# Masks over pairs of tiles, six of them in stage one, eight more split blocks and four kept blocks, in a two-layer graph kernel on one core

## Chip, cores and metric

One core of a Trainium2 chip runs the whole program. The metric is the device time of one execution in microseconds, lower is better.

## Reference

Two graph layers over 4096 nodes with 128 features, each followed by a residual and a layer norm without scale or shift. `adj` is 4096 x 4096, mostly zeros, with entries from 0.05 to 1.

```python
def reference(x, adj, L0_gnn_W1, L0_gnn_W2, L0_gnn_b, L1_gnn_W, L1_gnn_B):
    # layer 0:  K = 16 mixtures
    node = x @ W1                                  # (n, K)
    hw = einsum('nc,kcf->nkf', x, W2)
    x0 = einsum('nk,nkf->nf', node, hw)
    x1 = _layernorm(x + relu(adj @ x0 + node @ b))
    # layer 1
    msg = x1 @ W + B
    sens = exp(-(1.0 / adj - 1.0) ** 2 / 0.5)
    weights = where(adj < 1.0, sens, 0.0)
    return _layernorm(x1 + weights @ msg)
```

## The kernel before

Everything is kept transposed (features on partitions). `adj` is cut into 8 x 8 blocks of 512 x 512. It is read twice: as *row tiles* i = 0 to 63 (row r = i // 8, block g = i % 8) for `adj @ x0`, and as *weight tiles* t = 0 to 63 (column c = t // 8, block j = t % 8) for `weights @ msg`. Each tile is a 128 x 2048 array of 1 MB.

Stage one computes x0 for 8 groups of 512 nodes. TensorE makes the products `hw` in PSUM; for half of the chunks VectorE multiplies and adds them over k (`sum_over_k`, L861 and L864, PSUM and `part_acc` as operands), for the other half ScalarE scales them into `prods` (L600) and GpSimd adds these in a tree (`fold`, L1315, SBUF operands only). TensorE writes the first half's products into four banks, so it can be two quarters of a group ahead of VectorE. GpSimd also makes the remainder `x_lo` of the next group (L1323).

After that TensorE runs one fixed list of steps i. In each step it does row tile i and, 13 steps later than its own number (COL_LAG), column tile t = i - 13. A row tile is either four full-precision products (L451; two matmuls each, so eight in the profile) or, where `is_split` holds, *split*: VectorE rounds the tile to fp32r (`adj_hi`, L895) and subtracts (`row_lo`, L897), and TensorE does twelve one-pass matmuls (L440 to L442). `adj_hi` has two buffers, so `split_row_tile` waits until the row tile two splits back is done. When a row is complete, `node_bias` (L457) closes it, then come `residual` (L922), `centre` (L463 and L464 in two passes, L467 in full precision), `variance` (L473, L474 or L477), `scale_row` (L948), `messages` (L483), `copy_messages` (L966) and `add_row` (L957, a copy at L953 for kept blocks). For rows in ROWS_TWO_PASS, `round_row`, `remainder_of_row` (L934), `round_square` and `remainder_of_square` split the operands first.

A weight tile passes through VectorE `mask` (L909), then ScalarE `take_ln` (L616), `take_inverse` (L621), `take_square` (ScalarE L626, or VectorE L915 for every second pair) and `take_exp` (L633, L636). From tile 6 on, ScalarE works over two tiles at once. Column tiles of kept blocks add up in their own PSUM bank; for the others a shared bank is taken, and VectorE adds it to `sumT` (`add_part`, L974 a copy, L980 an addition).

The order on VectorE and ScalarE is a list of calls written out by hand. All loads go through SP's queue in a fixed order: row tile i + 5 once row tile i is done, weight tile t + 10 once column tile t is done; the weight slots 6 to 9 overlap stage one's arrays and are loaded after steps 2, 4, 7 and 9 (LATE_AT).

Of the kernel before, what the change touches and what calls it, by code (L numbers as in the profile page):

```python
# [5 lines left out]
F32 = mybir.dt.float32  # L6
# [5 lines left out]
P = 128  # L12
# [9 lines left out]
KEPT = 2  # L22
L1_BANKS = 2
# [5 lines left out]
SPLIT = (1, 3, 4, 5, 7)  # L29
SPLIT_FIRST = ((3, 5, 7), (1, 3, 5, 7))  # L30
SPLIT_LAST = (1, 3, 4, 5, 7)
# [10 lines left out]
ROWS_TWO_PASS = (2, 6)  # L42
# [23 lines left out]
def gnn_kernel(nc, adjT, xT, W1, W1T, W2, b0, WT, BT, outT):  # L66
# [23 lines left out]
    def is_split(i):  # L90
        if i // NB == NB - 1:
            return i % NB in SPLIT_LAST
        return i % NB in (SPLIT_FIRST[i // NB] if i < 2 * NB else SPLIT)

# [28 lines left out]

    def is_added(t):
        return t % NB >= KEPT or t >= TILES - NB

    def added_to(t):
        return len([s for s in range(t + 1) if is_added(s)])

# [7 lines left out]
    shared = [t for t in range(TILES) if t % NB >= KEPT]  # L137
# [10 lines left out]
    with ExitStack() as ctx:  # L148
# [9 lines left out]
        x0 = sb("x0", [P, NB * CH, P])  # L158
        if SPLIT:
            x0_hi = sb("x0_hi", [P, len(SPLIT) * CH, P], F32R)  # L160
            x0_lo = sb("x0_lo", [P, len(SPLIT) * CH, P], F32R)
# [44 lines left out]
        x1T = y  # L206
# [15 lines left out]
        yc_ps = psum("yc_ps", [P, BW])  # L222
        var_ps = psum("var_ps", [P, BW])
        small_ps = acc_ps[:, 1, P:4 * P].rearrange("p (n f) -> p n f", f=P)
        msg_ps = var_ps.rearrange("p (c f) -> p c f", f=P)
        shared_ps = [l1_ps[:, 0, :], l1_ps[:, 1, :], acc_ps[:, 0, :]]
        var2_banks = [var_ps[:, :], acc_ps[:, 1, :], yc_ps[:, :]]
# [85 lines left out]
        def _(sp):  # L313
# [34 lines left out]
            for g in (2, 3):  # L348
                load_x(g)
            for i in range(ROW_RING):  # L350
                load_row_tile(i)
            for t in range(WT_RING - LATE_SLOTS):
                load_wt(t)
# [25 lines left out]
        def _(pe):  # L379
# [48 lines left out]
            def row_tile(i):  # L428
                r, g = i // NB, i % NB
                acc = acc_ps[:, r % 2, :]  # L430
                if g == 0:
                    at_least(pe, y_made, r - 1)
                if is_split(i):
# [4 lines left out]
                    for c in range(CH):  # L438
# [3 lines left out]
                        mm = pe.matmul(acc, x0_lo[:, k, :], hi[:, c, :], start=False, stop=False)  # L442
# [16 lines left out]
            def centre(r):  # L459
                if row_in_two_pass(r):  # L460
                    pe.wait_ge(rounded_w_made, 2)
                    pe.wait_ge(y_lo_made, r - ROWS_TWO_PASS[0] + 1)
                    pe.matmul(yc_ps[:, :], centre_r[:, :], y_hi[:, :], start=True, stop=False)  # L463
                    pe.matmul(yc_ps[:, :], centre_r[:, :], y_lo[:, :], start=False, stop=True).then_inc(yc_made, 1)  # L464
                    return
                pe.wait_ge(y_made, r + 1)
                pe.matmul(yc_ps[:, :], centre_w[:, :], y[:, :], start=True, stop=True).then_inc(yc_made, 1)  # L467
# [11 lines left out]
            def messages(r):  # L479
                pe.wait_ge(x1_made, r + 1)  # L480
                pe.wait_ge(ln_var_made, r + 1)
                for c in range(CH):
                    mm = pe.matmul(msg_ps[:, c, :], x1T[:, c * P:(c + 1) * P], W_sb, start=True, stop=True)  # L483
                mm.then_inc(msg_made, 1)

            def col_tile(t):
# [3 lines left out]
                if j >= KEPT:  # L490
# [3 lines left out]
                    elif t >= THIRD_FROM:  # L494

                        pe.wait_ge(y_made, NB - 1)
                    out, first, last = shared_ps[bank_of[t]], True, True
                else:
                    out, first, last = kept_ps[:, j, :], c == 0, c == NB - 1
# [6 lines left out]
            def last_col_tile(half):  # L506

                pe.wait_ge(sum_added, added_to(before[LAST] if half == 0 else TILES - NB + 1))
# [27 lines left out]
            for i in range(LAST + COL_LAG):  # L536
# [7 lines left out]
                if g == 4 and 1 <= r < NB or i == TILES + 3:  # L544
# [4 lines left out]

                if g == 0 and 1 <= r <= NB and row_in_two_pass(r - 1):  # L550
# [14 lines left out]
        def _(act):  # L565
# [72 lines left out]
            def square(r):  # L638
                act.wait_ge(yc_made, r + 1)
                at_least(act, var_made, r)  # L640
                act.activation(sq[:, 0, :], yc_ps[:, :], ACT.Square).then_inc(sq_made, 1)
# [27 lines left out]
            round_x0(NB - 1)  # L669
            take_ln(0)  # L670
            take_inverse(0)
            take_square(0)
# [5 lines left out]
            square(0)  # L678
            take_exp(1)
            log_variance(0)  # L680
            take_inverse(2)
            inverse_root(0)
# [5 lines left out]
            take_ln(4)  # L688
            take_exp(3)
            take_inverse(4)  # L690
            take_square(4)
            take_ln(5)
            take_exp(4)
            take_inverse(5)
            take_square(5)
            take_ln(6)
            take_exp(5)
            take_inverse(6)
            square(1)
            take_square(6)  # L700
            take_ln(8)
            take_exp(6)
            log_variance(1)
            take_inverse(8)
            inverse_root(1)
            take_ln(10)
            take_inverse(10)
            take_exp(8)
            take_ln(12)
            take_square(10)  # L710
            take_inverse(12)
            take_exp(10)
            take_ln(14)
            take_exp(12)
            take_inverse(14)
            take_square(14)
            take_ln(16)
            square(2)
            take_exp(14)
            take_inverse(16)  # L720
            take_ln(18)
            log_variance(2)
            take_inverse(18)
            inverse_root(2)
            take_exp(16)
            take_ln(20)
            take_square(18)
            take_inverse(20)
            take_exp(18)
            take_ln(22)  # L730
            take_exp(20)
            take_inverse(22)
            take_square(22)
            take_ln(24)
            take_exp(22)
            square(3)
            take_inverse(24)
# [3 lines left out]
            take_exp(24)  # L741
            inverse_root(3)
            take_ln(28)
            take_square(26)
            take_inverse(28)
            take_exp(26)
            take_ln(30)
            take_inverse(30)
            take_exp(28)
            take_ln(32)  # L750
            take_square(30)
            take_inverse(32)
            square(4)
            take_exp(30)
            take_ln(34)
            take_exp(32)
            take_inverse(34)
            log_variance(4)
            take_square(34)
            inverse_root(4)  # L760
            take_exp(34)
# [600 lines left out]
```

## Time and profile before

| | before |
|---|---|
| time, median of 3 runs | 550.95 us (550.93 to 551.05) |
| the profiled execution: its time, its span | 552.33 us, 550.5 us |
| TensorE (PE) busy | 543.5 us, 99% |
| VectorE (DVE) busy | 497.3 us, 90% |
| ScalarE (ACT) busy | 497.2 us, 90% |
| GpSimd (POOL) busy | 83.3 us, 15% |
| mean DMA rate | 258 GB/s |

Busy shares are means over the span: GpSimd works in stage one alone (the first 104 us), ScalarE's weight work begins at 118.03 us. TensorE's matmuls are pipelined, and their modelled durations overlap, so tiles are measured here from one start to the next.

### The profile page before, as it was taken

How to read it: one execution, taken by the hardware profiler on the slowest of the kernel's cores; microseconds unless marked ns; L12 is line 12 of the kernel's file. 1: busy time of each engine (PE TensorE's matmuls, PEld its weight loads, DVE VectorE, ACT ScalarE, POOL GpSimd, SP SyncE). 2: the span in 40 equal slices, each digit the busy share in tenths (PEclk: the TensorE clock that was granted, in tenths of full speed). 3: DMA queues.
4: the chain of work that ended last, by engine and by line, in shares of the span. 5: the costliest groups of instructions: out<-in, count | busy, mean ns of one | idle time of the engine just before them, and what ended most of it. 6: DMA issues, size and time to landing. Idle time of an engine off the chain costs nothing.

```text
span 550.5 us, 5213 instructions
## 1 busy us (share of the span) xinstructions
PE 543.5 (99%) x1780; PEld 325.7 (59%) x1780; DVE 497.3 (90%) x564; ACT 497.2 (90%) x448; POOL 83.3 (15%) x76
## 2 busy tenths in 40 slices
PE   9999999999999999999999999999999999999996
PEld 7887888655655565556555655565555555554444
DVE  6686777999998799999989999999989998999997
ACT  5777888449999999989999999999999998999984
POOL 2888899400000000000000000000000000000000
PEclk9999999999999999999999999999999999999999
DMA  5992000299997888888888888887988796870003
GB/s 169 394 426 93 21 1 0 78 373 426 414 359 279 319 317 323 311 307 323 331 305 310 326 320 312 314 314 301 329 307 308 301 327 235 314 283 1 0 20 133
DMA packets 23130, 142.05 MB, mean 258 GB/s; under 512 B 2720, under 2 KB 3264, under 8 KB 6720
## 3 DMA queue, kind: packets, MB, share of 16 engines
q1 hardware_dynamic: 22960, 141.46, 68.5%
q8 instruction: 14, 0.23, 0.2%
q10 hardware_dynamic: 144, 0.26, 0.2%
q14 instruction: 12, 0.10, 0.1%
HBM read 139.62 MB, written 2.10 MB: 257 GB/s over the span
## 4 chain that ended last, share of the span: by engine, by line
PE 92%; DMA 4%; POOL 1%; issue 1%; ACT 1%; DVE 1%; DVEq 0%; ACTq 0%; POOLq 0%
PE l_ps L502 26%; PE acc_ps L451 17%; PE kept_ps L502 10%; PE acc_ps L442 6%; PE acc_ps L440 6%; PE acc_ps L441 6%; PE hw_ps L410 4%; DMA x_in<-xT_dram 4%; PE hw_ps L416 4%; PE hw_ps L413 4%; PE acc_ps L502 2%; PE var_ps L483 1%; PE acc_ps L457 1%; PE acc_ps L388 1%; POOL prods L1315 1%
## 5 line engine op out<-in xcount | busy, mean ns | idle before, releaser
L502 PE MATMUL l_ps<-wt_pair,msg 128*128 128x512 f32 x328 | 147.3, 592 | 0.0
L909 DVE SCALAR_TENSOR_TENSOR wt_pair<-wt_pair 128x2048 f32<-128x2048 f32 x60 | 136.5, 2285 | 3.5 <-DMA wt_pair<-adjT_dram 3.5
L616 ACT ACTIVATE wt_pair<-wt_pair 128x4096 f32<-128x4096 f32 (+1 forms) x33 | 109.0, 3302 | 10.9 <-DVE wt_pair L909 10.9
L621 ACT ACTIVATE wt_pair<-wt_pair 128x4096 f32<-128x4096 f32 (+1 forms) x33 | 109.0, 3302 | 0.3
L502 PEld LDWEIGHTS l_ps<-wt_pair,msg 128*128 128x128 f32 x328 | 61.7, 190 | 70.3 <-issue 69.2
L451 PE MATMUL acc_ps<-rows,x 128*128 128x512 f32 x216 | 96.8, 592 | 0.0
L600 ACT ACTIVATE prods<-hw_ps,node 128x128 f32<-128x128 f32 x256 | 73.1, 374 | 17.5 <-PE hw_ps L416 15.7
L897 DVE TENSOR_TENSOR row_lo<-rows,adj_hi 128x2048 fp32r<-128x2048 f32 x37 | 84.8, 2293 | 1.3
L864 DVE SCALAR_TENSOR_TENSOR part_acc<-hw_ps,node,part_acc 128x128 f32<-128x128 f32 x224 | 60.7, 343 | 21.1 <-PE hw_ps L416 21.1
L451 PEld LDWEIGHTS acc_ps<-rows,x 128*128 128x128 f32 x216 | 41.0, 190 | 50.1 <-issue 49.8
L440 PE MATMUL acc_ps<-adj_hi,x_hi 128*128 128x512 f32 x148 | 68.3, 462 | 0.0
L1315 POOL TENSOR_TENSOR prods<-prods 128x1024 f32<-128x1024 f32 (+2 forms) x45 | 66.4, 1477 | 10.8 <-ACT prods L600 8.3
L915 DVE SCALAR_TENSOR_TENSOR wt_pair<-wt_pair 128x4096 f32<-128x4096 f32 (+1 forms) x18 | 66.7, 3707 | 0.0
L442 PE MATMUL acc_ps<-adj_hi,x_lo 128*128 128x512 f32 x148 | 57.8, 391 | 0.0
L441 PE MATMUL acc_ps<-row_lo,x_hi 128*128 128x512 f32 x148 | 57.8, 390 | 0.0
L502 PE MATMUL kept_ps<-wt_pair,msg 128*128 128x512 f32 x128 | 57.4, 592 | 0.0
L633 ACT ACTIVATE wt_pair<-wt_pair 128x4096 f32<-128x4096 f32 (+1 forms) x18 | 54.8, 3043 | 1.6 <-DVE wt_pair L915 1.6
L895 DVE CAST adj_hi<-rows 128x2048 fp32r<-128x2048 f32 x37 | 45.2, 1222 | 11.4 <-PE acc_ps L442 9.4
L626 ACT ACTIVATE wt_pair<-wt_pair 128x4096 f32<-128x4096 f32 (+1 forms) x18 | 54.9, 3050 | 0.3
L636 ACT ACTIVATE wt_pair<-wt_pair 128x4096 f32<-128x4096 f32 (+1 forms) x18 | 54.7, 3041 | 0.0
L410 PE MATMUL hw_ps<-W_hi,x_hi 128*128 128x512 f32 x128 | 50.9, 397 | 1.2 <-ACT prods L600 1.2
L416 PE MATMUL hw_ps<-W_lo,x_hi 128*128 128x512 f32 x128 | 50.0, 391 | 0.0
(117 smaller groups left out, 554.7 us busy)
## 6 DMA issues: line engine op xcount, KB each, us to landing
rows<-adjT_dram SPq DMA_DIRECT2D x68, 1024.0 KB, 4.9
wt_pair<-adjT_dram SPq DMA_DIRECT2D x60, 1024.0 KB, 4.8
x_in<-xT_dram SPq DMA_DIRECT2D x8, 256.0 KB, 3.9
x_row<-xT_dram SPq DMA_DIRECT2D x8, 256.0 KB, 5.1
outT_dram<-sumT SPq DMA_DIRECT2D x7, 256.0 KB, 2.0
W_in<-W_dram SPq DMA_DIRECT2D x3, 256.0 KB, 4.5
W_in<-W_dram ACTq DMA_DIRECT2D x1, 256.0 KB, 3.7
outT_dram<-sumT SPq DMA_DIRECT2D x2, 128.0 KB, 1.9
```

Of the source, the lines that this page charges most:

```text
L410: pe.matmul(out, x_hi[:, s, nodes], W2_hi[:, ks, :], start=True, stop=False)
L416: pe.matmul(out, x_hi[:, s, nodes], W2_lo[:, ks, :], start=False, stop=True).then_inc(hw_made[half], 1)
L440: pe.matmul(acc, x0_hi[:, k, :], hi[:, c, :], start=(g == 0 and c == 0), stop=False)
L441: pe.matmul(acc, x0_hi[:, k, :], lo[:, c, :], start=False, stop=False)
L442: mm = pe.matmul(acc, x0_lo[:, k, :], hi[:, c, :], start=False, stop=False)
L451: mm = pe.matmul(acc, x0[:, g * CH + c, :], row_in[i % ROW_RING][:, c, :], start=(g == 0 and c == 0), stop=False)
L502: mm = pe.matmul(out, msg[:, c % 2, k, :], wt[t][:, k, :], start=(first and k == 0), stop=(last and k == CH - 1))
L600: op = act.activation(prods[:, c2, k, :], hw_ps[1][:, n % HW_BANKS[1], kk, :], ACT.Copy, scale=node[:, s, HALF + c2, k:k + 1])
L616: act.activation(w, w, ACT.Ln, bias=TINY).then_inc(ln_made, 1)
L621: act.activation(w, w, ACT.Exp, scale=-1.0).then_inc(inv_made, 1)
L897: dve.tensor_tensor(flat(lo[:, :, :]), flat(whole[:, :, :]), flat(hi[:, :, :]), ALU.subtract).then_inc(adj_lo_made, 1)
L909: dve.scalar_tensor_tensor(out=w, in0=w, scalar=1.0, in1=w, op0=ALU.is_lt, op1=ALU.mult).then_inc(made, 1)
```

## The change

Masks of tiles 6 to 59 are made over two tiles by one instruction (`mask_pair`). Masks 0 to 5 move into stage one, each behind a `sum_over_k`; the first six weight tiles are therefore loaded ahead of the first five row tiles. Block 6 is split in rows 1 to 7 and block 4 in row 1 too. Four blocks (the even ones) are kept in PSUM instead of two, which leaves one shared bank instead of two; the centred row `yc_ps` moves into the accumulator bank of its row, and kept rows are scaled straight into `sumT`, without an `add_row`. Row 1 gets the two-pass centring and variance. The messages of two-pass rows come behind the column tile of their step. Some remainders of x0 are stored in place of x0. The orders on VectorE and ScalarE are new.

```diff
-KEPT = 2
-L1_BANKS = 2
+KEPT = 4
+L1_BANKS = 1
-SPLIT = (1, 3, 4, 5, 7)
-SPLIT_FIRST = ((3, 5, 7), (1, 3, 5, 7))
-SPLIT_LAST = (1, 3, 4, 5, 7)
+SPLIT = (1, 3, 4, 5, 6, 7)
+SPLIT_FIRST = ((3, 5, 7), (1, 3, 4, 5, 6, 7))
+LO_APART = (1, 4, 6)
+SIXTH, SIXTH_ROWS = 6, (2, 3, 4, 5, 6)
+SPLIT_LAST = (1, 3, 4, 5, 6, 7)
-ROWS_TWO_PASS = (2, 6)
+ROWS_TWO_PASS = (1, 6)
...
+    def is_kept(j):
+        return j % 2 == 0
...
-            for i in range(ROW_RING):
-                load_row_tile(i)
             for t in range(WT_RING - LATE_SLOTS):
                 load_wt(t)
+            for i in range(ROW_RING):
+                load_row_tile(i)
...
                 if g == 0:
-                    at_least(pe, y_made, r - 1)
+                    at_least(pe, x1_made, r - 1)
...
-                if g == 4 and 1 <= r < NB or i == TILES + 3:
+                if (g == 4 and 1 <= r < NB and not row_in_two_pass(r - 1)) or i == TILES + 3:
                     messages(r - 1)
                 t = i - COL_LAG
                 if t >= 0:
                     col_tile(t)
+                if g == 4 and 1 <= r < NB and row_in_two_pass(r - 1):
+                    messages(r - 1)
...
+            def mask_pair(m):
+                w = weights(m)
+                for t in (m, m + 1):
+                    dve.wait_ge(wt_in[t % WT_RING], 16 * (t // WT_RING + 1))
+                dve.scalar_tensor_tensor(out=w, in0=w, scalar=1.0, in1=w, op0=ALU.is_lt,
+                                         op1=ALU.mult).then_inc(mask_made, 2)
...
             def add_part(t):
-                part_ps = shared_ps[bank_of[t]] if j >= KEPT else kept_ps[:, j, :]
+                part_ps = kept_ps[:, j // 2, :] if is_kept(j) else shared_ps[bank_of[t]]
...
             for g in range(NB):
                 sum_over_k(g)
...
+                if 1 <= g <= FIRST_PAIR:
+                    mask(g - 1)
```

VectorE's new order, from the first row's residual to row 1's end, and around column tile 25:

```python
residual(0); mask_pair(6); split_row_tile(11); split_row_tile(12); scale_row(0); split_row_tile(13)
mask_pair(8); copy_messages(0); split_row_tile(14); split_row_tile(15); split_row_tile(17); add_part(1)
split_row_tile(19); residual(1); mask_pair(10); round_row(1); take_square(8); remainder_of_row(1); add_part(3)
round_square(1); mask_pair(12); split_row_tile(20); remainder_of_square(1); add_part(5)
split_row_tile(21); take_square(12); scale_row(1); split_row_tile(22); add_row(1); copy_messages(1)
mask_pair(14); split_row_tile(23); add_part(7)
...
split_row_tile(37); scale_row(3); mask_pair(30); add_row(3); split_row_tile(38); copy_messages(3); take_square(28)
add_part(23); split_row_tile(39); mask_pair(32); split_row_tile(41); residual(4); mask_pair(34); round_row(4); add_part(25)
```

ScalarE's new order has the same calls for the weight tiles, with some exponentials and squares behind the next logarithms, and begins with `take_ln(0)`, `take_inverse(0)` ahead of the last `round_x0`.

## Rows read from the trace of the kernel before

**Rows 1.** The page's chain that ended last, share of the span by engine.
```profile
PE 92%; DMA 4%; POOL 1%; issue 1%; ACT 1%; DVE 1%; DVEq 0%; ACTq 0%; POOLq 0%
```
**Rows 2.** Stretches: length, busy us of PE, PEld, DVE, ACT, POOL; clock, DMA share, GB/s.
```profile
60.00:100.00 40.00, 40.00 (x189) 33.44 (x189) 29.36 (x110) 33.65 (x119) 37.02 (x31) 1.00 0.03 8
130.00:150.00 20.00, 20.00 (x71) 12.43 (x70) 17.91 (x12) 18.78 (x13) 0.00 (x0) 1.00 1.01 417
...
217.71:271.83 54.12, 54.12 (x163) 29.99 (x163) 52.19 (x35) 52.67 (x18) 0.00 (x0) 1.00 0.86 316
```
**Rows 3.** The chain in order of time: start us, us, engine, tile and line.
```profile
149.70 3.43 PE kept_ps L502 x8
...
160.00 0.23 PE acc_ps L440
...
162.73 0.86 PE acc_ps L457 x2
...
197.61 0.89 PE var_ps L483 x8
...
228.87 0.23 PE yc_ps L463
```
**Rows 4.** VectorE's timeline, 235 to 251: start us, us, line, operation, shapes.
```profile
235.66 0.42 DVE L939 CAST sq_rounded<-sq 128x512 fp32r<-128x512 f32 x1
236.00 0.68 DVE L980 TENSOR_TENSOR sumT<-l_ps,sumT 128x512 f32<-128x512 f32 x1
236.60 0.68 DVE L943 TENSOR_TENSOR rstd_rounded<-sq,sq_rounded 128x512 fp32r<-128x512 f32 x1
237.20 2.28 DVE L909 SCALAR_TENSOR_TENSOR wt_pair<-wt_pair 128x2048 f32<-128x2048 f32 x1
239.40 4.42 DVE L915 SCALAR_TENSOR_TENSOR wt_pair<-wt_pair 128x4096 f32<-128x4096 f32 x1
243.74 0.68 DVE L980 TENSOR_TENSOR sumT<-l_ps,sumT 128x512 f32<-128x512 f32 x1
...
246.54 1.22 DVE L895 CAST adj_hi<-rows 128x2048 fp32r<-128x2048 f32 x1
...
250.00 0.68 DVE L948 TENSOR_TENSOR y<-yc_ps,rstd 128x512 f32<-128x512 f32 x1
```
**Rows 5.** VectorE's timeline, residual(0) and split 15, with the wait before it.
```profile
129.25 0.68 DVE L922 SCALAR_TENSOR_TENSOR y<-acc_ps,x_row 128x512 f32<-128x512 f32 x1
...
149.30 1.23 DVE L895 CAST adj_hi<-rows 128x2048 fp32r<-128x2048 f32 x1 [1.16 <-DMA rows<-adjT_dram]
```
**Rows 6.** SP's timeline: issues of weight tile 9, then row tiles 15 to 18.
```profile
135.98 0.43 SPq L322 DMA_DIRECT2D wt_pair<-adjT_dram  x1
139.90 10.16 SPq L318 DMA_DIRECT2D rows<-adjT_dram  x4
```
**Rows 7.** GpSimd: its widest fold among the groups by form, and two folds' starts.
```profile
L1315 POOL TENSOR_TENSOR prods<-prods 128x1024 f32<-128x1024 f32 x15 | 36.0, 2403 | 8.4 <-ACT prods L600 8.3
...
57.17 4.59 POOL L1315 TENSOR_TENSOR prods<-prods 128x1024 f32<-128x1024 f32 x3 [1.21 <-ACT prods L600]
...
69.20 4.58 POOL L1315 TENSOR_TENSOR prods<-prods 128x1024 f32<-128x1024 f32 x3 [0.57 <-ACT prods L600]
```
**Rows 8.** VectorE's timeline in stage one, around the ends of two groups.
```profile
56.83 0.60 DVE L864 SCALAR_TENSOR_TENSOR x<-hw_ps,node,part_acc 128x128 f32<-128x128 f32 x2
58.05 0.61 DVE L861 TENSOR_SCALAR part_acc<-hw_ps,node 128x128 f32<-128x128 f32 x2 [0.62 <-PE hw_ps L416]
58.58 1.63 DVE L864 SCALAR_TENSOR_TENSOR part_acc<-hw_ps,node,part_acc 128x128 f32<-128x128 f32 x6
...
68.66 0.60 DVE L864 SCALAR_TENSOR_TENSOR x<-hw_ps,node,part_acc 128x128 f32<-128x128 f32 x2
```
**Rows 9.** TensorE's timeline: the fifth step of the group that follows.
```profile
62.00 0.49 PE L410 MATMUL hw_ps<-W_hi,x_hi 128*128 128x512 f32 x1
```
**Rows 10.** Waits of TensorE, the longest: us in total, times, longest.
```profile
PE hw_ps L410 <- ACT prods L600: 1.2, 1, 1.2
```

More of the change, by code:

```diff
@@ L204, in gnn_kernel @@
         rstd_rounded = sb("rstd_rounded", [P, 2, BW], F32R)
-        x1T = y
+        x1T = [block_of(sumT, q) if is_kept(q) else y[:, :] for q in range(NB)]
         msg = sb("msg", [P, 2, CH, P])
@@ L1079, in _ @@
+            remainder_of_row(1)
             add_part(3)
+            round_square(1)
+            mask_pair(12)
             split_row_tile(20)
-            add_part(4)
-            mask(13)
-            mask(14)
+            remainder_of_square(1)
             add_part(5)
-            take_square(8)
+            split_row_tile(21)
+            take_square(12)
             scale_row(1)
-            split_row_tile(21)
+            split_row_tile(22)
             add_row(1)
-            add_part(6)
@@ L1107, in _ @@
-            split_row_tile(28)
-            round_square(2)
-            add_part(12)
-            remainder_of_square(2)
-            mask(21)
-            take_square(16)
+            mask_pair(16)
+            residual(2)
+            add_part(9)
+            round_row(2)
+            mask_pair(18)
+            remainder_of_row(2)
+            split_row_tile(27)
+            take_square(16)
+            round_square(2)
+            split_row_tile(28)
+            remainder_of_square(2)
+            add_part(11)
@@ L1138, in _ @@
-            add_part(20)
-            remainder_of_square(3)
-            take_square(24)
-            mask(29)
+            mask_pair(28)
             add_part(21)
-            mask(30)
             split_row_tile(37)
             scale_row(3)
-            add_part(22)
+            mask_pair(30)
             add_row(3)
+            split_row_tile(38)
+            copy_messages(3)
+            take_square(28)
+            add_part(23)
             split_row_tile(39)
-            copy_messages(3)
@@ L1177, in _ @@
             copy_messages(4)
+            add_part(31)
+            take_square(36)
             split_row_tile(47)
-            add_part(31)
-            add_row(4)
-            mask(40)
-            take_square(36)
+            mask_pair(40)
             split_row_tile(49)
-            mask(41)
-            mask(42)
+            residual(5)
+            add_part(33)
+            round_row(5)
             split_row_tile(51)
-            add_part(34)
-            mask(43)
-            residual(5)
@@ L1234, in _ @@
-            add_row(6)
+            split_row_tile(62)
+            add_part(47)
             copy_messages(6)
-            add_part(46)
             split_row_tile(63)
-            add_part(47)
+            mask_pair(56)
             take_square(52)
-            mask(56)
+            add_part(49)
             take_square(54)
-            mask(57)
+            residual(7)
+            mask_pair(58)
             take_square(55)
-            mask(58)
-            residual(7)
             mask(60)
-            mask(59)
```

385 lines of the change are left out of this document (180 added, 205 removed).

## Prediction

> **What bounds the kernel now.** I read the page's chain first: TensorE holds 92% of it [rows 1], so a TensorE microsecond saved counts unless something else becomes late. Then the table by stretch [rows 2], for what stands next. In one row of blocks (217.71 to 271.83, from one bias product to the next) TensorE is busy all 54.12 us, VectorE 52.19 and ScalarE 52.67, so a shorter TensorE period soon meets two queues that are nearly full. In stage one (60 to 100) TensorE is full, VectorE has 29.4 of 40 and GpSimd 37.0 of 40. Between 130 and 150 the DMA engines are full at 417 GB/s. The clock is 1.00 throughout. Last come the timelines, which give the prices: a full-precision tile costs TensorE 3.43 us (eight matmuls), a split tile 162.73 - 160.00 = 2.73, four message products 0.89, a bias product 0.86 [rows 3]. On VectorE I take start to start, since ends overlap the next start by some 0.08: mask of one tile 2.20, operation over a pair of tiles 4.34, split 3.46, a 512-wide two-operand operation 0.60, a rounding 0.34 [rows 4].
>
> **TensorE's work.** Split blocks go from 37 to 45: row 1 gains blocks 4 and 6, rows 2 to 6 gain block 6, row 7 gains block 6. 8 x (3.43 - 2.73) = 5.6 us removed. Row 1's centring and variance become two-pass: a full-precision product of that form takes 0.86, a two-pass one about 0.47 (two of 0.23) [rows 3], twice 0.39 = 0.8. In all 6.4 us less.
>
> **VectorE's work.** 27 pair masks replace 54 single ones: 2 x 2.20 - 4.34 = 0.06 each [rows 4], 1.6 in all. The nearest row for a pair mask is the pair square L915, same operation class and shape. The Trainium skill (VectorE: DVE Perf Modes, Side-by-side) gives each operation a fixed part of some 158 cycles, by which halving the count would save 0.165 us a pair, 4.4 in all; the starts in the trace show that most of it already lies under its neighbour. Four kept blocks take 14 add_parts away (8.4 us) and four add_rows (about 2 us). Eight splits add 27.7, row 1's roundings and remainders 1.9, one more remainder of x0 0.6. Six masks (13.2 us) leave the rows for stage one. Per row in rows 2 to 6: one split more (3.46), pair masks -0.24, two add_parts fewer -1.2, half an add_row fewer -0.3, so +1.7: 52.2 becomes 53.9 against a TensorE period of 54.1 - 0.7 = 53.4. VectorE now has 0.5 us too much per row, paid from the masks' lead, of which row 1 eats 6.9 + 1.9 + 0.6. So capacity is just there, and the fixed order decides. ScalarE's work is unchanged apart from one rounding, and it can start at the end of stage one, because masks 0 to 5 are then made; at 52.7 a row it keeps that lead. I put its effect at nothing: its cover is the lead, and without it the price is the part of the 6.4 us that it fails to follow.
>
> **Where the new order makes TensorE wait.** I laid the new VectorE queue beside the TensorE queue. split_row_tile waits until the row tile two splits back is done, so at several places VectorE starts from a TensorE event; from there both sides are sums.
> - Column tile 0 waits for copy_messages(0), which is now behind mask_pair(8), which needs weight tile 9. That load is issued right ahead of row tile 15 (135.98 and 139.90) [rows 6], and row tile 15 keeps VectorE waiting until 149.30 [rows 5]; at 417 GB/s [rows 2] one megabyte less is 2.5 us earlier, 146.8. VectorE is there before: from residual(0) at 129.25 [rows 5], 0.60 + 4.34 + three splits + 0.60 is 145.2. Then 146.8 + 4.34 + 0.7 = 151.8, where TensorE comes at 149.70 - 0.70 = 149.0 [rows 3]: 2.8 us. Without the load it would be about 1.2.
> - centre(1), now two-pass, needs remainder_of_row(1). From the end of row tile 15: split 19, residual, mask pair, rounding, pair square, remainder = 3.46 + 0.60 + 4.34 + 0.34 + 4.34 + 0.68 = 13.8; TensorE: bias 0.86 and three tiles of 3.43 = 11.15. Wait 2.6.
> - Column tile 9 needs the one shared bank free, that is add_part(7). From row tile 19: three splits, a pair square, a pair mask, scale, add_row, copy, add_part = 10.4 + 8.7 + 2.5 = 21.5; TensorE: three column tiles, three split tiles, messages = 10.3 + 8.2 + 0.9 = 19.4. Wait 2.1.
> - Column tile 27 needs add_part(25). From row tile 35: four splits, three pair masks, a pair square, six small ones, a rounding = 13.8 + 13.0 + 4.3 + 3.7 + 0.3 = 35.2; TensorE: five column tiles, four split, one full, messages, bias = 33.2. Wait 1.9 to 2.0.
> These make 9.5 (bounds 5 to 12: each is a difference of long sums, good to about 0.8). Elsewhere I found VectorE in time by 0.2 us or more. Behind each wait stands all of TensorE's queue, and the weight and row loads behind that. The rows thus end 9.5 - 6.4 = 3.1 later.
>
> **Six masks in stage one.** Each follows sum_over_k and delays the next block's first quarter. VectorE has 0.62 us idle before that quarter (58.05) and the quarter takes 2.16 [rows 8]; TensorE next needs it for its fifth step at 62.00 [rows 9]. A mask from 57.35 ends at 59.6, the quarter at 61.8: hidden with 0.2 to spare. But GpSimd works there too. No row shows it beside a VectorE operation with both operands in SBUF: in stage one VectorE reads one operand from PSUM. Lower bound 0 (they run side by side). Upper bound, if one must wait for the other: GpSimd's 2.40 us fold [rows 7] starts at 57.17, before the mask could, and lets it go at 59.6; the quarter ends at 64.0 and TensorE loses 2.0, times six 12, less the 1.2 that TensorE waits there anyway [rows 10]: 10.8. In four of the six blocks VectorE would be first by 0.02 (69.18 against 69.20) [rows 7, 8]; then GpSimd is 2.2 late with 0.9 idle per block (3.0 of 40 [rows 2], blocks of 12 [rows 7]), which TensorE sees through ScalarE as 0 to 1.3; I take 0.25. So 2 x 2.0 - 1.2 + 4 x 0.25 = 3.8, between the ends because the races fall on both sides.
> The Trainium skill (SBUF — State Buffer, Who interferes with whom) says that a VectorE instruction with two SBUF inputs contends with a GpSimd instruction that reads SBUF, one blocking the other for its whole length. By that rule the term lies between 3.8 and 10.8, without it at 0 to 0.3; no run here shows it yet.
>
> **Sum.** -6.4 + 9.5 + 3.8 = +6.9, rounded +7. The profiled execution took 552.33 us with a span of 550.5; it stands 1.4 above the median 550.95. The change applied to the median: 558.0.
>
> **Rivals.**
> - Side by side: stage one costs nothing, the four waits stand. 550.95 + 3.1 = 554. For it: VectorE's small operations and GpSimd's folds already overlap without either being longer; against it: those have only one operand in SBUF.
> - Faster: VectorE keeps ahead. The waits hang on VectorE being at the foot of each sum no later than TensorE's event and on weight tile 9; if VectorE's queue were one split further on (3.46) at each place, by the lead of the moved masks, the last three vanish and the first shrinks to 1.2 or less. Then 550.95 - 6.4 + 1.2 = 545.8, or 544.6 with none left. It decides where the waits sum to under 6.4. For it: the lead exists. Against it: the double buffer of split tiles makes VectorE wait for TensorE, and a mask cannot be pulled forward in a fixed order.
> - Waits gone but exclusion in force: 544.6 + 3.8 = 548.4, up to 555.
> - Full exclusion in all six blocks and the waits: 550.95 + 3.1 + 10.8 = 565.
> - ScalarE becomes the bound: 52.7 of 53.4 per row says no by 0.7 a row; if so, the gain would be cut to what it follows, at most 6.4, so about 551.
>
> **Chances.** Forecast (556 to 562) 0.40; side by side (552 to 556) 0.25; full exclusion (562 to 566) 0.10; faster with no exclusion 0.14; waits gone with exclusion 0.07; ScalarE 0.04. Measurement tells about 0.2% (1.1 us) from no change. Faster than 549.8: 0.14 + 0.05 = 0.19; within: 0.06; slower: 0.75. Leaving out the lower half of the faster case and the top of exclusion, the range is 546 to 565; where the sign is as forecast, 552 to 565.
>
> **What would show it.** The chain after should have TensorE waits at L502 for copy_messages L966 near 149 after an unchanged stage one, at L463 for the remainder L934 in row 1, and at L502 for add_part L980 in rows 2 and 4; some 2 us each. In stage one GpSimd's folds would start 2 us late or be longer, or masks would start late; if folds and masks keep their durations and their starts, exclusion is refuted. Period of a row 53.4. I am wrong if TensorE's waits in the rows come to under 6 us, or if L909 pair masks take much other than 4.34.

## The result, and the profile after

| | before | after |
|---|---|---|
| median of 4 runs, us | 551.0 | 574.8 (570.99 to 575.58) |
| ratio, 95% interval | | 1.042 (1.037 to 1.046) |
| profiled execution, us | 552.33 | 570.99 |
| its span, us | 550.5 | 569.2 |
| its mean granted clock | 1.00 | 0.989 |

The change makes the kernel 4.2% slower: 23.8 us, where 7 were forecast. The profiled execution is the quickest of the four after; the other three have mean clocks of 0.983 to 0.987. Four executions stand far outside the rest and count in no ratio below: one of e1 (634.55 us, the one with a trace, so e14 repeats e1), one of e2 (1834.97), one of e9 (1136.42) and one of the kernel before beside e9 to e12 (628.45).

The page's chain, share of the span by engine, beside [rows 1]:

```profile
PE 56%; DVE 20%; issue 12%; POOL 7%; DMA 2%; ACT 2%; DVEq 0%; SPq 0%; ACTq 0%
```

TensorE held 92% and now holds 56%; VectorE and GpSimd have come onto the chain. The table by stretch, in the columns of [rows 2]:

```profile
60.00:100.00 40.00, 34.35 (x160) 27.54 (x159) 29.81 (x97) 29.26 (x104) 38.27 (x29) 1.00 0.03 8
130.00:150.00 20.00, 20.00 (x63) 11.52 (x62) 17.05 (x12) 19.31 (x13) 0.00 (x0) 1.00 1.01 417
```

In stage one TensorE lost 5.65 of 40 us while GpSimd rose from 37.0 to 38.3. What TensorE waited for, all executions of a line together (us in total, times, longest):

```profile
PE hw_ps L434 <- ACT prods L626: 6.3, 5, 2.7
PE acc_ps L487 <- DVE rstd_rounded L967: 2.9, 1, 2.9
PE hw_ps L434 <- DVE part_acc L890: 2.1, 2, 1.7
PE l_ps L526 <- DVE sumT L1004: 2.0, 1, 2.0
PE kept_ps L526 <- DVE msg L996: 1.8, 1, 1.8
PE l_ps L526 <- DVE sumT L1012: 1.7, 1, 1.7
```

Two of the rows (L434) are stage one, 8.4 us in all, where the kernel before waited 1.2 [rows 10]. The other four are the forecast waits in the rows, each at its forecast place, 8.4 us in all. On TensorE's timeline:

```profile
160.53 5.40 PE L526 MATMUL kept_ps<-wt_pair,msg 128*128 128x512 f32 x8 [1.84 <-DVE msg L996]
...
188.85 0.77 PE L487 MATMUL acc_ps<-sq_rounded,centre_r 128*128 128x512 f32 x1 [2.85 <-DVE rstd_rounded L967]
...
228.85 5.40 PE L526 MATMUL l_ps<-wt_pair,msg 128*128 128x512 f32 x8 [1.96 <-DVE sumT L1004]
...
353.67 3.70 PE L526 MATMUL l_ps<-wt_pair,msg 128*128 128x512 f32 x8 [1.72 <-DVE sumT L1012]
```

Two of the column tiles that follow a wait take 5.40 us; the third, and every undisturbed one, takes 3.6 to 3.7 by the same column (3.43 from start to start, [rows 3]). The stretches of 2 us around the first and the last of these waits say why (the eighth field is the granted clock):

```profile
160.00:162.00 2.00, 1.47 (x3) 0.71 (x4) 1.97 (x3) 2.00 (x2) 0.00 (x0) 0.76 0.99 410
162.00:164.00 2.00, 2.00 (x4) 0.94 (x3) 2.00 (x2) 2.00 (x2) 0.00 (x0) 0.50 0.92 385
164.00:166.00 2.00, 2.00 (x6) 0.77 (x5) 1.97 (x2) 2.00 (x1) 0.00 (x0) 0.89 0.08 33
...
354.00:356.00 2.00, 2.00 (x6) 0.84 (x5) 1.97 (x3) 2.00 (x1) 0.00 (x0) 1.00 1.03 438
```

Behind the wait of 1.84 the granted clock is 0.50, the 1.2 GHz level instead of 2.4, and it returns a few microseconds later; behind the wait of 1.72 it stays 1.00. The waits of 2.85 and 1.96 are followed by a fall of the same size. Adding up what the clock is short of 1.00, each of the three falls takes 1.7 us, which is what the column tiles show (5.40 instead of 3.70): 5.1 in all, of which 0.25 at the second still lies inside the wait. A mean clock of 0.989 over 569.2 us would be 6.3 us, but the other 1.2 lie at the very end, where TensorE has nothing left to do:

```profile
567.00:568.00 1.00, 0.00 (x0) 0.00 (x0) 0.02 (x1) 0.00 (x0) 0.00 (x0) 0.61 0.65 224
568.00:569.20 1.20, 0.00 (x0) 0.00 (x0) 0.00 (x0) 0.00 (x0) 0.00 (x0) 0.50 0.25 83
```

Stage one ends where the first full-precision row tiles start, before above after:

```profile
102.13 10.46 PE L451 MATMUL acc_ps<-rows,x 128*128 128x512 f32 x24
```

```profile
111.36 10.46 PE L475 MATMUL acc_ps<-rows,x 128*128 128x512 f32 x24
```

The account for the profiled execution, against a difference in span of 569.2 - 550.5 = 18.7: stage one later by 111.36 - 102.13 = 9.2, waits in the rows 8.4, clock 5.1, TensorE's work -6.4: 16.3. The 2.4 left are not placed one by one; 0.8 of it lies behind the last row's bias product. The 9.2 is good to some 2 us: in the traces of kernels whose folds all keep their length, the first row tile starts between 100.64 (e6) and 103.75 (e15). The median lies 3.8 higher than this execution, with lower clocks.

### The profile page after: what moved, and what is told of

It reads as the page before. It is cut to its first block, busy times and chain, and to the rows that moved or that the text cites. A ratio compares the mean times of both kernels' runs of the same rounds, so it can differ in the third digit from the quotient of the medians.

```text
span 569.2 us, 5272 instructions
## 1 busy us (share of the span) xinstructions
PE 546.1 (96%) x1812; PEld 332.5 (58%) x1812; DVE 513.7 (90%) x540; ACT 497.6 (87%) x449; POOL 95.5 (17%) x76
## 4 chain that ended last, share of the span: by engine, by line
PE 56%; DVE 20%; issue 12%; POOL 7%; DMA 2%; ACT 2%; DVEq 0%; SPq 0%; ACTq 0%
PE l_ps L526 11%; PE kept_ps L526 11%; PE acc_ps L475 9%; POOL prods L1311 6%; DVE wt_pair L942 5%; DVE wt_pair L948 4%; PE acc_ps L464 4%; PE acc_ps L465 4%; PE acc_ps L466 4%; DVE adj_hi L921 3%; PE hw_ps L434 3%; PE hw_ps L440 3%; PE hw_ps L437 2%; DMA wt_pair<-adjT_dram 2%; ACT prods L626 2%
## 5 line engine op out<-in xcount | busy, mean ns | idle before, releaser
L642 ACT ACTIVATE wt_pair<-wt_pair 128x4096 f32<-128x4096 f32 (+1 forms) x33 | 108.9, 3301 | 16.3 <-DVE wt_pair L942 16.3
L942 DVE SCALAR_TENSOR_TENSOR wt_pair<-wt_pair 128x4096 f32<-128x4096 f32 x27 | 119.2, 4417 | 0.0
L526 PE MATMUL kept_ps<-wt_pair,msg 128*128 128x512 f32 x240 | 110.0, 601 | 2.1 <-DVE msg L996 1.8
L923 DVE TENSOR_TENSOR row_lo<-rows,adj_hi 128x2048 fp32r<-128x2048 f32 x45 | 103.2, 2292 | 1.5
L526 PE MATMUL l_ps<-wt_pair,msg 128*128 128x512 f32 x216 | 99.0, 602 | 3.7 <-DVE sumT L1004 2.0
L464 PE MATMUL acc_ps<-adj_hi,x_hi 128*128 128x512 f32 x180 | 81.4, 452 | 0.2 <-DVE row_lo L923 0.2
L526 PEld LDWEIGHTS kept_ps<-wt_pair,msg 128*128 128x128 f32 x240 | 45.6, 192 | 54.0 <-issue 48.8
L526 PEld LDWEIGHTS l_ps<-wt_pair,msg 128*128 128x128 f32 x216 | 41.4, 192 | 52.0 <-issue 46.1
L465 PE MATMUL acc_ps<-row_lo,x_hi 128*128 128x512 f32 x180 | 70.6, 392 | 0.0
L475 PE MATMUL acc_ps<-rows,x 128*128 128x512 f32 x152 | 68.0, 592 | 0.0
L434 PE MATMUL hw_ps<-W_hi,x_hi 128*128 128x512 f32 x128 | 51.7, 404 | 8.4 <-ACT prods L626 6.3
L437 PE MATMUL hw_ps<-W_hi,x_lo 128*128 128x512 f32 x128 | 49.9, 390 | 0.0
```

Source lines behind the costliest of these rows:

```text
L464: pe.matmul(acc, x0_hi[:, k, :], hi[:, c, :], start=(g == 0 and c == 0), stop=False)
L465: pe.matmul(acc, x0_hi[:, k, :], lo[:, c, :], start=False, stop=False)
L475: mm = pe.matmul(acc, x0[:, g * CH + c, :], row_in[i % ROW_RING][:, c, :], start=(g == 0 and c == 0), stop=False)
L526: mm = pe.matmul(out, msg[:, c % 2, k, :], wt[t][:, k, :], start=(first and k == 0), stop=(last and k == CH - 1))
L642: act.activation(w, w, ACT.Ln, bias=TINY).then_inc(ln_made, 1)
L923: dve.tensor_tensor(flat(lo[:, :, :]), flat(whole[:, :, :]), flat(hi[:, :, :]), ALU.subtract).then_inc(adj_lo_made, 1)
```

## Experiments

Two theories stood against each other. **Locks, order and clock:** (1) in stage one VectorE's masks and GpSimd's folds hold each other up; (2) the waits in the rows come from the order of the hand-written lists; (3) the clock falls behind some waits and multiplies both. **Load:** VectorE simply has too much to do, in stage one and in the rows, so that time moved is time lost. Ratios are to the kernel before, timed on the same chip; a ratio of 1.01 is 5.5 us.

### Stage one: e1, e14, e8

e1 and e14 are one kernel, the kernel before with only this (and `mask(0)` to `mask(5)` taken out of VectorE's list):

```diff
-            for i in range(ROW_RING):
-                load_row_tile(i)
             for t in range(WT_RING - LATE_SLOTS):
                 load_wt(t)
+            for i in range(ROW_RING):
+                load_row_tile(i)
...
+                if 1 <= g <= FIRST_PAIR:
+                    mask(g - 1)
```

> The kernel before with only one part of the change: the first six weight tiles are loaded ahead of the row tiles, and their masks (two operands in SBUF) run in stage one, one behind each of the sums over k of blocks 1 to 6. Theory (VectorE's two-SBUF-operand masks and GpSimd's folds hold each other up): stage one ends about 9.4 us later as in the changed kernel, masks of 3.9 and folds of 6.5 to 6.7 appear, the rows gain nothing since TensorE was full there: 551.0 + 9.4 = 560 us (558 to 562). Rival (the changed kernel's stage one is late for another reason, such as its other buffers or its PSUM banks): 551 us, folds all at 4.6.

> The kernel before with the six masks in stage one alone, a second time, for a trace with TensorE's clock at its usual level. Theory: TensorE waits 8 to 9 us in stage one (folds of 6.4 to 6.7 beside the masks); where one of these waits is 2 us or longer the granted clock can fall to 0.50 behind it, some 2 us each time, so the time is before + 9 with the clock at 1.00 and up to before + 15 without. Rival (the clock has no part in it): every run within 1 us of before + 9.4.

Measured: e1 1.023 (1.016 to 1.029), e14 1.024 (1.019 to 1.029), some 13 us. e14's executions took 563.3 and 563.4 at clocks of 0.997 and 0.998, and 566.4 and 568.2 at 0.991; e1's three others 561.4 at a clock of 1.000, 563.3 at 0.997 and 568.5 at 0.991. So the moved masks alone, with the loads in their new order, cost more than half of the change's loss, and the clock has its part. GpSimd's folds and VectorE's mask in e14 (a group of folds is three instructions, 4.59 in [rows 7]):

```profile
47.62 6.71 POOL L1311 TENSOR_TENSOR prods<-prods 128x1024 f32<-128x1024 f32 x3 [2.17 <-ACT prods L600]
...
56.08 6.72 POOL L1311 TENSOR_TENSOR prods<-prods 128x1024 f32<-128x1024 f32 x3
```

```profile
59.93 2.28 DVE L909 SCALAR_TENSOR_TENSOR wt_pair<-wt_pair 128x2048 f32<-128x2048 f32 x1
```

The group of folds that starts at 56.08 is still at work when the mask runs from 59.93 to 62.2; the mask takes its usual 2.28 and the folds last 2.1 longer. All six masks have such a fold beside them (6.47 to 6.72); the first mask is itself held up, 3.90 instead of 2.28. TensorE then waits 2.72 us for ScalarE, which waited for GpSimd to free `prods`, and its clock in stretches of 5 us is

```profile
60.00:65.00 5.00, 2.28 (x11) 1.58 (x10) 4.28 (x10) 1.56 (x6) 4.92 (x3) 1.00 0.00 0
65.00:70.00 5.00, 5.00 (x19) 4.16 (x18) 2.16 (x8) 3.31 (x13) 4.76 (x6) 0.62 0.01 2
70.00:75.00 5.00, 5.00 (x17) 3.95 (x17) 1.69 (x7) 2.14 (x8) 4.38 (x4) 0.70 0.17 52
```

e14's wait of 1.69 at 38.83 is followed by a fall too, its wait of 2.74 at 95.13 by none. In the changed kernel's profile the same wait of 2.72, at 62.97, is followed by a clock of 1.00, as are all its waits in stage one. So one and the same wait sometimes costs the clock and sometimes not, which fits the scatter of these kernels by 5 us: e14's two falls take 1.7 and 3.4.

e8 keeps masks 3 to 5 in the rows:

```diff
+                if 1 <= g <= 3:
+                    mask(g - 1)
```

> The run with the masks alone moved, with only the masks of tiles 0 to 2 in stage one (behind blocks 1 to 3); those of 3 to 5 stay in the rows. Theory (each mask pays for itself): folds of 6.4 to 6.8 only in blocks 1 to 3 and 4.6 in the others, and half of the cost of six masks, 4 to 5.5 us over before. Rival (the cost comes from GpSimd falling behind once and for all, so the first masks are free or the first one costs all): under 2 or over 8 us.

Measured 1.014 (1.009 to 1.018), 7.5 us: just over half of e14's 13, and more than the 4 to 5.5 expected. The profiled execution (562.8) has the same two falls of the clock as e14's; the other three took 557.9 to 558.3. Folds of 6.47, 6.71 and 6.71 up to 58 us, and 4.54 to 4.61 in all later ones. Each mask pays for itself.

### What in the mask does it: e2, e13, e15

All three leave the masks in the rows and put other work of VectorE on the same six weight tiles at the same six places of stage one, with the loads in the new order (in e13 and e15 a tile's mask in the rows then waits for this work).

```diff
+                dve.tensor_reduce(out=spare[:, t:t + 1], in_=flat(wt[t]), op=ALU.max,
+                                  axis=mybir.AxisListType.X)                                   # e2
+                dve.tensor_scalar(flat(wt[t]), flat(wt[t]), 1.0, None, ALU.mult).then_inc(scaled, 1)   # e13
+                dve.tensor_scalar(flat(wt[t]), flat(wt[t]), 1.0, 0.0, ALU.mult, ALU.add,
+                                  accum_out=spare[:, t:t + 1]).then_inc(scaled, 1)   # e15
```

> As the run before, but the masks stay in the rows, and at their six places in stage one VectorE does a maximum over the same weight tile instead: same 2048 elements a partition, one SBUF operand, result into one column. It is work that the reference doesn't ask for. Theory of two SBUF operands: no fold gets longer than 4.6, stage one as in the kernel before, 551 us (to 551.5). Rival 1 (VectorE's time itself, or weight loads ahead of the row tiles, delays stage one): about 560 us as with the masks. In between if only part of it is the lock.

> As the run with a maximum at six places of stage one, but VectorE multiplies the weight tile by 1.0 there, in place: one SBUF operand, and all 2048 elements a partition written back, as by a mask. It is work that the reference doesn't ask for; the masks stay in the rows. Theory (the second SBUF operand is what holds GpSimd up): folds of 4.6 and the time of the kernel before, within 0.4%. Rival (writing a whole tile in SBUF is what holds it up, and the maximum escaped because it writes one column): folds of 5.8 to 6.7 beside it, 3 us or more over before.

> The run that multiplied the weight tiles by 1.0 in place had VectorE in a faster way of working: 1.22 us where a mask takes 2.28. Here the same multiplication also writes the sum over each partition into a spare column, which should keep it at one element a cycle, some 2.3 us: one SBUF operand, the whole tile written back, no double rate. Theory (what holds GpSimd is an operation that takes in more than one SBUF element a cycle, be it as a second operand or at the double rate): folds of 4.6 and before + 1 at most. Rival (writing a whole tile back holds it, for as long as the operation takes): folds of 6.4 to 6.7 and 8 us or more over before, as with the masks. If it runs at 1.2 us all the same, folds of 5.6 would leave the two apart from each other unsettled.

| | VectorE's operation | SBUF operands | written | its time | folds beside it | ratio (interval) |
|---|---|---|---|---|---|---|
| e14 | mask | 2 | all | 2.28 (the first 3.90) | 6.47 to 6.72 | 1.024 (1.019 to 1.029) |
| e2 | maximum | 1 | one column | 2.28 | 4.59 | 1.003 (1.001 to 1.005) |
| e13 | times 1.0 | 1 | all | 1.22 to 1.24 (the first 2.84) | 5.42 to 5.66; two of the six meet a group's fourth and last fold, 1.32 instead of 0.46 | 1.008 (1.006 to 1.010) |
| e15 | times 1.0, summed | 1 | all | 2.27 | 4.55 to 4.61 | 1.003 (1.001 to 1.005) |

The groups of GpSimd's widest fold, e13 above e15 (count, then busy, mean ns), against 2403 in [rows 7]:

```profile
L1324 POOL TENSOR_TENSOR prods<-prods 128x1024 f32<-128x1024 f32 x15 | 39.1, 2609 | 6.0 <-ACT prods L601 6.0
```

```profile
L1325 POOL TENSOR_TENSOR prods<-prods 128x1024 f32<-128x1024 f32 x15 | 36.1, 2405 | 7.6 <-ACT prods L602 7.5
```

e2 refutes "VectorE's time": the same 2.28 us at the same places lengthen no fold. e13 then broke the narrow form of the theory: one SBUF operand, and yet the folds grow by 1.05, about as long as the operation lasts. It runs at twice the elements per microsecond (2048 in 1.22 instead of 2.28). e15 writes as much at the single rate and lengthens nothing, so writing is not it either. What fits all four: VectorE holds GpSimd up when it takes in two SBUF elements at a time, as a second operand or at the double rate, and for the length of the operation. This is what the Trainium skill (SBUF — State Buffer, Who interferes with whom) states: two SBUF inputs contend with a GpSimd instruction that reads SBUF, a copy or `tensor_scalar` in a two-port mode does too, a reduction does not; whoever comes first holds the shared ports for its whole instruction. All four runs agree with it: folds of 6.47 to 6.72 beside two operands, 5.42 to 5.66 beside the double rate, 4.59 beside the reduction, 4.55 to 4.61 beside the single rate. The 0.3% that e2 and e15 are slower is not placed: 0.4 us of it is one wait of TensorE for `part_acc` in stage one, and some 1.0 lies behind stage one (449.4 us from the first row tile to the end in both, 448.4 in the kernel before); they also have the new load order.

### The wait and the clock: e5, e6

The kernel before, with one mask (e5) or two (e6) moved ahead of `copy_messages(0)`, and nothing else:

```diff
             mask(6)
+            mask(7)
+            mask(8)                       # e6 alone
             copy_messages(0)
             split_row_tile(15)
-            mask(7)
             split_row_tile(17)
-            mask(8)                       # e6 alone
```

> The kernel before with copy_messages(0) put behind the mask of weight tile 7. In the kernel before its result is there at 148.1 and TensorE comes for it at 149.5; a mask takes 2.2, so TensorE should wait 0.8 us ahead of column tile 0. Theory (the clock falls only behind the longer waits): the granted clock stays 1.00 in the stretch behind it, the column tile takes 3.4 to 3.6, and the kernel 0.8 us more than the kernel before. Rival (any wait halves the clock): some 2 us more than the kernel before and a column tile of 5.4.

> The same with copy_messages(0) behind the masks of weight tiles 7 and 8, nothing else changed: TensorE should wait about 3 us ahead of column tile 0. Theory: behind it the granted clock is 0.5 for some microseconds, the column tile takes 5.4 instead of 3.6, and the kernel is 4.5 to 6 us slower than before, more than its wait. Rival (the clock's fall in the changed kernel comes from its heavier VectorE work and not from the wait): the clock stays 1.00 and the kernel is 3 us slower.

e5: ratio 1.001 (0.999 to 1.003). e6: 1.009 (1.006 to 1.012), 5.1 us for a wait of 3.0. Column tile 0 in each, e5 above e6:

```profile
151.52 3.70 PE L502 MATMUL kept_ps<-wt_pair,msg 128*128 128x512 f32 x8 [0.83 <-DVE msg L966]
```

```profile
151.24 5.08 PE L502 MATMUL kept_ps<-wt_pair,msg 128*128 128x512 f32 x8 [3.03 <-DVE msg L966]
```

Behind the wait of 0.83 the clock stays 1.00; behind that of 3.03 it is 0.66 and then 0.50 in two stretches of 2 us, and the column tile takes 1.4 more. A kernel with none of the change's load shows it, so the fall needs a wait and not the load; e10 below shows that a wait alone does not settle it.

### Mending the order by hand: e3, e7, e4

e3 moves VectorE's calls at the four waits, e7 at two more places that e3 showed:

```diff
-            mask_pair(8)
             copy_messages(0)
             split_row_tile(14)
+            mask_pair(8)
...
-            mask_pair(10)
             round_row(1)
-            take_square(8)
             remainder_of_row(1)
+            mask_pair(10)
+            take_square(8)
... (add_part(7) behind copy_messages(1), add_part(25) behind residual(4))
-            round_square(1)            # e7
             mask_pair(12)
-            split_row_tile(20)
+            round_square(1)
             remainder_of_square(1)
+            split_row_tile(20)
... (add_part(11) behind take_square(16))
```

> The changed kernel with VectorE's order changed at the four places where TensorE waited: copy_messages(0) and split 14 ahead of the pair mask of tiles 8 and 9; the remainder of row 1 ahead of the pair mask of tiles 10 and 11 and the pair square; add_part(7) right behind copy_messages(1); add_part(25) right behind residual(4). Theory (the waits cost about 9.2 us and TensorE's clock falls to half behind the longer ones, 5 to 10 us more): both go, 574.8 - 9.2 - 5 to 10 = 556 to 561, mean clock 0.997 or more. Rival 1 (the clock falls for another reason, for instance the load on the chip): 565.6, clock still 0.985 to 0.989. Rival 2 (the moved operations make others late): new waits of 2 us each at other places, 565 or more.

> The run with four waits mended, and two more places changed where it showed new ones: the rounding and remainder of square 1 behind the pair mask of tiles 12 and 13 and ahead of split 20 (TensorE waited 2.8 for the remainder), and add_part(11) right behind the pair square of tiles 16 and 17 (TensorE waited 2.3 for it). Theory (waits and the clock behind them are all that the rows lose): 5.1 us of waits and some 3 us of clock go, 568.5 - 8 = 560 us, span about 557, clock 0.998 or more; what is left over before is stage one, +9.4 - 6.4 = +3 and 1 to 2 at small waits and at the end. Rival (VectorE is simply too full: 53.9 of 53.4 a row, so a wait mended comes back somewhere else): 565 us or more, with new waits of 2 us.

Measured: e3 1.031 (1.027 to 1.034), e7 1.031 (1.027 to 1.035). Of 4.2% each won 1.1%, and e7 nothing over e3; both lie well above what was expected of them (556 to 561 and 560 us). The mended waits shrank or went, and others came: in e3 2.8 for the remainder of square 1 and 2.3 for `add_part(11)`, in e7

```profile
214.16 1.91 PE L507 MATMUL var_ps<-small,y 128*128 128x128 f32 x8 [3.63 <-DVE y L981]
```

because VectorE reached the pair square ahead of `scale_row(1)` before ScalarE had its inverse, and stood 4.49 us there. Taken alone these two runs speak for "load".

e4 puts the six masks back into rows 0 and 1 and leaves all else as changed:

```diff
-                if 1 <= g <= FIRST_PAIR:
-                    mask(g - 1)
...
             remainder_of_x0(1)
+            mask(0)
             split_row_tile(7)
... (masks 1 to 5 between the calls up to mask_pair(6); ScalarE's order there as before)
```

> The changed kernel with the masks of weight tiles 0 to 5 back in row 0 and row 1 of the rows (ScalarE's order at its start as in the kernel before), all else as changed. Theory: stage one is 9.4 us shorter and ends where the kernel before ends it; VectorE has 13.2 us more in the first rows, where it has no lead, so the first waits of TensorE grow: 565 us if they stay as they are, up to 575 if all 13 us are paid by the path. Rival (stage one's delay has nothing to do with the masks): stage one still ends at 111 us.

Measured 1.036 (1.032 to 1.039): stage one is again full, and TensorE waits 8.4 us at column tile 0 instead, where `copy_messages(0)` now stands behind 13 us more of masks.

### Another order throughout: e9, e10, e11, e12

Here both lists behind stage one were laid out anew: the traces' durations laid end to end on each engine with every wait, and calls moved by a few places until TensorE stood as little as possible. e9 is the whole change with some 50 of VectorE's 220 calls in another place, for example around row 1 (several calls to a line here; + is e9):

```diff
-            residual(1)  mask_pair(10)  round_row(1)  take_square(8)  remainder_of_row(1)
-            add_part(3)  round_square(1)  mask_pair(12)  split_row_tile(20)  remainder_of_square(1)
+            residual(1)  add_part(1)  round_row(1)  mask_pair(10)  remainder_of_row(1)  split_row_tile(19)
+            take_square(8)  mask_pair(12)  add_part(3)  round_square(1)  remainder_of_square(1)  split_row_tile(20)
```

e10 has the masks back in the rows. e11 and e12 also make fewer new splits:

```diff
-SPLIT_FIRST = ((3, 5, 7), (1, 3, 4, 5, 6, 7))
-SIXTH, SIXTH_ROWS = 6, (2, 3, 4, 5, 6)
+SPLIT_FIRST = ((3, 5, 7), (1, 3, 5, 7))
+SIXTH, SIXTH_ROWS = 6, (4, 5, 6)       # e12: (), and SPLIT_LAST without 6
```

> The changed kernel, all its parts kept (six masks in stage one, six split blocks, four kept blocks, pair masks), but VectorE's and ScalarE's lists behind stage one put in another order: the same calls, moved by a few places wherever, with the durations of the traces laid end to end, TensorE came out waiting. By those sums TensorE waits some 3 us in the rows, none over 1.6, and the rows take 3.3 us less than in the kernel before. Theory (the waits are the order's, not VectorE's load): before + 9.4 in stage one - 3.3 = before + 6 us, ratio about 1.011, clock 0.997 or more. Rival (VectorE is too full with six split blocks, so any order ends in waits): ratio 1.025 or more as in the two runs with mended waits.

> The same with the six masks back in the rows: VectorE has 13.2 us more there, stage one is that of the kernel before. Laid end to end, TensorE waits some 7 us, most of it in rows 0 and 1 (the longest 2.2 ahead of row tile 13), and the rows take 2.7 us more than in the kernel before. Theory: ratio about 1.005 (before + 2.7 us), plus what the clock loses behind a wait of 2. Rival (as in the run with masks back in the rows in the given order: the 13 us come out on TensorE's path): ratio 1.03.

> What the other runs point to: pair masks, four kept blocks and the two-pass centring of row 1 stay; the six masks stay in the rows; of the eight new splits only four are made (block 6 in rows 4, 5, 6 and 7); lists in an order laid out as in the run before. Removed from TensorE: 4 x 0.70 + 0.8 = 3.6 us; VectorE gets 4 x 3.46 more and 12 less. Laid end to end, 1.6 us of small waits stay. Theory: 2.5 us faster than the kernel before, ratio 0.9955. Rival (waits that the sums don't see): same or slower than before.

> The parts of the change that relieve VectorE, without those that load it: pair masks, four kept blocks (one shared bank), row 1 two-pass; no new splits (37 as before), the masks in the rows, lists in an order laid out as above. Theory: TensorE's work falls by 0.8 only, and nothing waits: ratio 0.9975 to 0.9985. Rival (one shared bank for the odd blocks and the pair masks themselves make TensorE wait): ratio over 1.003.

| | ratio | interval | us, 551.0 x (ratio - 1) |
|---|---|---|---|
| e9, all of the change | 1.019 | 1.014 to 1.024 | +10.6 |
| e10, masks in the rows | 1.004 | 1.001 to 1.006 | +2.0 |
| e11, four new splits | 0.996 | 0.994 to 0.998 | -2.3 |
| e12, no new splits | 0.998 | 0.997 to 1.000 | -0.9 |

e9's waits of TensorE in the rows came to 2.0 us. That it lies above its forecast of +6 is stage one and its clock:

```profile
90.00:100.00 10.00, 7.26 (x28) 5.67 (x27) 6.20 (x17) 4.87 (x17) 9.69 (x8) 0.80 0.00 0
100.00:110.00 10.00, 10.00 (x40) 8.15 (x39) 6.34 (x17) 7.03 (x26) 6.27 (x5) 0.86 0.00 0
```

Its rows begin 7.3 us later than the changed kernel's. Two falls of the clock in stage one, behind its waits of 1.69 and 2.74, take 5.1 of it:

```profile
118.63 10.46 PE L475 MATMUL acc_ps<-rows,x 128*128 128x512 f32 x24
```

From there to the end of its span of 563.7 it takes 445.1 us. The kernel before takes 448.4 for the same (102.13 to 550.5) and the changed kernel 457.8 (111.36 to 569.2): the same calls in another order are 12.7 us shorter, and 3.3 shorter than the kernel before, as expected. By ratio e9 is 0.5%, some 2.6 us, under e14, which has the masks alone, but those two intervals overlap. e10 carries every mask in the rows and all eight new splits, and is 3.2% quicker than e4, the same work in the given order. So VectorE is not too full; e3 and e7 mended places one by one in lists that have to fit as a whole. e10 does have waits of 2.1 and 1.9 in the first rows, and its column tile behind the second took 5.40 again; behind the first the clock stayed 1.00:

```profile
150.75 0.47 PE L464 MATMUL acc_ps<-adj_hi,x_hi 128*128 128x512 f32 x1 [2.12 <-DVE row_lo L923]
...
155.60 5.40 PE L526 MATMUL kept_ps<-wt_pair,msg 128*128 128x512 f32 x8 [1.86 <-DVE msg L996]
```

e11 is the one version whose interval lies below the kernel before, by 0.4%: 3.6 us of TensorE's work removed, no wait in the rows or at the end over 0.8. e12's interval reaches 1.000.

## Why the prediction was off

- **The sign, and the rows' structure:** right. The four waits came where the sums put them; 2.8, 2.6, 2.1 and 1.9 to 2.0 were forecast, 1.84, 2.85, 1.96 and 1.72 measured, 8.4 against 9.5. One cause was misnamed: at column tile 0 the pair mask did not wait for weight tile 9's load; split 13 ahead of it had waited 1.64 us until row tile 11 was done, and only then did `mask_pair(8)` start, at 155.45.
- **TensorE's work, -6.4:** right as far as a run shows it. One undisturbed row of the changed kernel, from one bias product to the next, takes 290.27 - 236.84 = 53.43, where 53.4 was forecast for 54.1:

```profile
236.84 1.02 PE L481 MATMUL acc_ps<-x_row,small 128*128 128x512 f32 x2
...
290.27 1.02 PE L481 MATMUL acc_ps<-x_row,small 128*128 128x512 f32 x2
```

  e11 removes 3.6 by the same prices and gained 2.3 (1.3 to 3.2), with 1.9 us of small waits in the rows and at the end where the kernel before has 0.7.
- **Pair masks:** 4.42 us each, as the pair square in [rows 4]. The 0.06 saved per pair is not measured by itself; e12, with all that relieves VectorE, is at 0.998 (0.997 to 1.000).
- **The step that failed first: four of the six blocks at 0.25 each, in the 3.8 of stage one.** Stage one measured 9.2 without any clock. The exclusion was forecast, and its upper bound of 10.8 held. The race went even further VectorE's way than I had it: one mask of six was held up (3.90), the other five kept their 2.28. What failed is that I then treated GpSimd's lateness as nearly free. GpSimd has 0.9 us idle in a block of 12 [rows 2]; a mask makes the folds beside it some 2.1 longer, and what exceeds the 0.9 goes on through `prods` and ScalarE to TensorE: 6.3 of the 8.4 us wait came that way. Six times 2.1 - 0.9 is 7.2, and TensorE's waits in stage one rose by 7.2, from 1.2 to 8.4. The price should have been near the upper bound for all six.
- **The step that was missing: the clock.** "The clock is 1.00 throughout" was read from a kernel whose longest TensorE wait is 1.2 [rows 10] and carried over to one with waits of 2 to 3. It cost 5.1 us in the profiled execution, and the lower mean clocks of the others say more there. e6 shows it: a wait of 3.0 cost 5.1 (3.4 to 6.8), and its column tile took 1.4 more than e5's. With the clock the rows came out 9.4 later (457.8 against 448.4), where 3.1 were forecast.
- **Rivals:** side by side is refuted by the folds of 6.47 to 6.71. Full exclusion, 565, is nearest; it lacks the clock. ScalarE never became the bound: it idled 16.3 us for pair masks.
- With the two steps put right, 550.95 - 6.4 + 8.4 + 9.2 is 562, and 5.1 to 8.5 of clock make 567 to 571 (5.1 from the trace; the other executions' mean clocks are up to 0.006 lower, 3.4 us by estimate). The 4 to 8 us from there to the median are the 2.4 that are not placed and what the other executions, of which there is no trace, lost besides; that split is argued, not shown.

## What to carry to other kernels

Before moving VectorE work beside GpSimd work, ask whether it takes in two SBUF elements at a time (two SBUF operands, or the double rate); if so, add about its length to GpSimd's queue and follow what is left of GpSimd's idle time to the engine that waits for it. Price a stall of TensorE of some 2 us or more at its length, plus up to 1.7 us for half clock behind it as in these rows (3.4 in e14's stage one), and read the clock in the changed kernel, not in the one before. Where two hand-written lists feed one engine, lay the whole of both out against it before judging capacity: the same work differed by 3% in two orders (e4 and e10), and mending the worst waits singly brought back a quarter of the loss.

## What the runs showed of the hardware that was not expected

A one-operand multiplication in place at the double rate (1.22 us) holds GpSimd's folds up by 1.05 to 1.07; the same at the single rate (2.27 us) does not. The length of TensorE's wait does not settle whether the granted clock falls to 0.50 behind it. In the rows of all traces but e1's it fell at all seven waits of 2.31 or more, at 1.84, 1.86 (e10), 1.95 (e4) and 1.96, and not at 1.93 (e4), 2.12 (e10), 1.72 and less. In stage one the wait of 1.69 was followed by a fall in e8, e9 and e14 and by none in the changed kernel, e3 and e7, and of eleven waits of 2.71 to 2.74 three were. What decides is open.
